# Attention and ternary FFN kernel: the product with v split in two pieces in steps without other matmul blocks

## The reference

```
q, k, v = x Wq' + bq, x Wk' + bk, x Wv' + bv      16 heads of 16
q, k    = rope(q) / 4, rope(k)
a       = softmax(q k') v                          per head, over 1024 keys
x       = layernorm(x + a Wo' + bo)
x       = layernorm(x + relu(x Q(W1)' + b1) Q(W2)' + b2)
```

## Time and profile before

| | us |
|---|---|
| runs: median (lowest to highest) | 3323.97 (3323.8 to 3325.73) |
| profiled execution: span from first to last instruction | 3316.4 |
| profiled execution: time around the span | not given by the page; the median of the runs is 7.5 above the span |
| PE busy | 3242.7 |
| DVE busy | 2990.2 |
| ACT busy | 2530.5 |
| POOL busy | 2147.2 |

### The profile page before, as it was taken

One profiled execution on the slowest core, in us unless ns is written; L12 is line 12 of the kernel. 1 busy time (PEld: TensorE's weight loads), 2 busy tenths in 40 slices (PEclk: granted clock), 3 DMA queues, 4 the chain that ended last, 5 costly groups with the idle time before them and its releaser, 6 DMA issues. The chain is left out here.

```text
span 3316.4 us, 81549 instructions
## 1 busy us (share of the span) xinstructions
PE 3242.7 (98%) x30726; PEld 1773.5 (53%) x30726; DVE 2990.2 (90%) x5721; ACT 2530.5 (76%) x4971; POOL 2147.2 (65%) x2440
## 2 busy tenths in 40 slices
PE   7989999999999999999999999999999999999997
PEld 4434555555555555555555555555555555544445
DVE  7888999999999999999999999999999999999965
ACT  3777777777777777777777777777777777777773
POOL 2575766766766766766766766766766776754435
PEclk7999999999999999999999999999999999999989
DMA  8444454454355345355355345345345345344211
GB/s 220 100 96 103 96 116 103 96 116 107 93 115 109 91 115 111 89 115 111 94 114 118 88 109 118 92 105 119 94 106 116 96 104 116 98 95 80 55 38 57
DMA packets 312553, 341.20 MB, mean 103 GB/s; under 512 B 77280, under 2 KB 260448, under 8 KB 312160
## 3 DMA queue, kind: packets, MB, share of 16 engines
q1 hardware_dynamic: 311584, 335.20, 44.2%
q10 hardware_dynamic: 576, 0.79, 0.2%
HBM read 195.37 MB, written 140.51 MB: 101 GB/s over the span
## 5 line engine op out<-in xcount | busy, mean ns | idle before, releaser
L1071 DVE TENSOR_REDUCE mxp<-ms 128x1 f32<-128x512 f32 x4064 | 2614.6, 681 | 245.5 <-PE ms L749 200.7
L897 ACT ACTIVATE prob<-sc 128x512 f32<-128x512 f32 x4096 | 2225.1, 597 | 655.4 <-PE sc L760 629.6
L760 PE MATMUL sc<-qa,ka 50*128 50x512 f32 x4096 | 1545.2, 444 | 27.5 <-ACT prob L897 27.1
L749 PE MATMUL ms<-ka,qa 48*128 48x512 f32 x4064 | 1536.7, 446 | 2.9 <-DVE mxp L1289 2.2
L760 PEld LDWEIGHTS sc<-qa,ka 50*128 50x128 f32 x4096 | 684.5, 185 | 1115.8 <-ACT prob L897 962.6
L777 PE MATMUL ob<-prob,v_sb 128*17 128x512 f32 x8192 | 1081.9, 600 | 2.4 <-ACT at_st L904 2.3
L749 PEld LDWEIGHTS ms<-ka,qa 48*128 48x128 f32 x4064 | 679.4, 185 | 10.4 <-DVE mxp L1071 4.5
L1402 POOL TENSOR_TENSOR ve<-mv,eps_sb 128x2 f32<-128x2 f32 x119 | 23.2, 195 | 493.1 <-DVE mv L1098 493.1
L1423 POOL TENSOR_TENSOR hid_r<-hid,hid_r 128x512 fp32r<-128x512 f32 x240 | 308.6, 1286 | 19.2
L777 PEld LDWEIGHTS ob<-prob,v_sb 128*17 128x17 f32 x8192 | 136.0, 95 | 258.4 <-issue 258.1
L597 PEld LDWEIGHTS job<-h_t,w_sb 64*128 64x128 f32 x3840 | 261.3, 186 | 23.4
(11 more groups left out here) (157 smaller groups left out, 2833.6 us busy)
## 6 DMA issues: line engine op xcount, KB each, us to landing
qk_parts<-parts SPq DMA_DIRECT2D x122, 512.0 KB, 4.2
ka<-qk_parts SPq DMA_DIRECT2D x378, 128.0 KB, 4.6
qa<-qk_parts SPq DMA_DIRECT2D x378, 128.0 KB, 7.4
attention<-at_st SPq DMA_DIRECT2D x128, 256.0 KB, 3.3
v_ones<-v_st SPq DMA_DIRECT2D x64, 272.0 KB, 2.4
v_sb<-v_ones SPq DMA_DIRECT2D x64, 272.0 KB, 8.5
xn<-x SPq DMA_DIRECT2D x64, 256.0 KB, 4.8
ao<-attention SPq DMA_DIRECT2D x128, 128.0 KB
```

Of the source, the lines that this page charges most:

```text
L749: nc.tensor.matmul(ms[upto(b, g, NS1, at) % MS_BANKS][:, :], operand(qa, b, g, j, ROWS)[:, qt * P:(qt + 1) * P], operand(ka, b, g, j, ROWS ...
L760: nc.tensor.matmul(sc[upto(b, g, HG * STEPS, n) % SC_BANKS][:, :], operand(ka, b, g, j, ROWS + MROWS)[:, tt * P:(tt + 1) * P], operand(qa, ...
L897: nc.scalar.activation(prob[st_ % 2][:, j, :], sc[upto(b, g, HG * STEPS, n) % SC_BANKS][:, :], ACT.Exp).then_inc(s["exp_done"], 1)
L1071: nc.vector.reduce_max(mxp[(b * G + g) % 2][:, kh, j * TT + qt:j * TT + qt + 1], ms[upto(b, g, NS1, at) % MS_BANKS][:, :], AX.X).then_inc( ...
```

## The change

In steps that have no job, W is made in two pieces of 256 queries each, the first behind S1 and the second behind S3. In steps with a job the order stays S0 S1 job S2 S3 W. Each piece has the four heads' matmuls with half the columns and loads the same v tile again. The `start` flag of an accumulation is set on the first piece alone, `stop` on the second; `pv_done` is told by the second piece. The waits at the head of `weigh` stand ahead of each piece.

```diff
-            def weigh(b, g, st_):
+            def weigh(b, g, st_, begin=0, end=NQ):
...
                 for j in range(HG):
-                    last = nc.tensor.matmul(ob[32 * j:32 * j + VW, :], v_sb[g % 2][:, tt, j, :], prob[st_ % 2][:, j, :],
-                                            start=(tt == 0), stop=(tt == TT - 1))
-                last.then_inc(s["pv_done"], 1)
-
-            def weigh_before(b, g, st_, first):
+                    last = nc.tensor.matmul(ob[32 * j:32 * j + VW, begin:end], v_sb[g % 2][:, tt, j, :], prob[st_ % 2][:, j, begin:end],
+                                            start=(tt == 0 and begin == 0), stop=(tt == TT - 1 and end == NQ))
+                if end == NQ:
+                    last.then_inc(s["pv_done"], 1)
+
+            def weigh_before(b, g, st_, first, begin, end):
 
                 if st_ > 0:
-                    weigh(b, g, st_ - 1)
+                    weigh(b, g, st_ - 1, begin, end)
                 elif not (first and g == 0):
-                    weigh(b + (g - 1) // G, (g - 1) % G, STEPS - 1)
+                    weigh(b + (g - 1) // G, (g - 1) % G, STEPS - 1, begin, end)
...
-                            if j == (3 if jobs else 1):
-                                weigh_before(b, g, st_, first)
+                            if jobs and j == 3:
+                                weigh_before(b, g, st_, first, 0, NQ)
+                            elif not jobs and j % 2 == 1:
+                                weigh_before(b, g, st_, first, j // 2 * (NQ // 2), (j // 2 + 1) * (NQ // 2))
```

## The result

| | before | after |
|---|---|---|
| median, us (lowest to highest) | 3324.85 (3323.8 to 3327.86), 4 runs | 3301.19 (3298.73 to 3303.37), 4 runs |
| profiled execution, us | not given | 3303.37 |
| its span, us | 3316.4 | 3301.6 |

The ratio is 0.9934, with a 95% interval of 0.9922 to 0.9947: faster by 0.7%.

The account below looks back on a forecast made before the run. PE and ACT take turns, neither full, with the whole product on their ring in 58 jobless steps. Gains of 8.0 (batch 0), 8.0 (five late groups) and 1.5 (last group) make 17.5 us: 3324.0 to 3306.5, range 3300 to 3316.

Parts of the forecast that it names:

- rival (c): Steps 5 to 8 of (15,3): denser steps may keep the clock up, time 3300.5 us; chance 0.08.
- Ring and price of a piece: PE-ACT cycle in jobless steps: 3.08 us falls to 2.65 a step, as a half piece costs 0.55 against 0.98 whole.
- Rival (b): Jobless steps: a piece costs 0.65 us, second piece adds 0.10 per step, time 3311; chance 0.21 together with rival (a).
- rival (d): Jobless steps: halving saves nothing, a piece takes 0.98 us, steps 0.2 longer, time 3335.5; chance 0.04.
- Rival (e): Jobless steps: an unseen wait keeps the score chain from being let go earlier, time 3321 to 3326 us; chance 0.07.
- the fixed part: Each piece of the product: 0.12 us that does not go with the clock, beside 0.43 for a half piece's columns.
- Batch 0 up to the gate: Jobless runs from (0,0) step 6 through (0,2) step 1: 3.7 us gained.
- The gate: Start of (0,3): POOL and the maxima's DMA cap the gain at 0 to 1 us, 0.4 taken; then 0.7 for steps 0-1.
- The five late groups: Groups (14,2) to (15,2): 1.6 us gained each, 8.0 in all, transposition in step 6 gated by POOL's norm.
- rival (a): Other engines take more: late groups 0.65 us each, batch 0 DMA waits give nothing, time 3312; chance 0.21 with rival (b).
- (15,3): Last group: 1.3 us from three steps before the clock halves, 0.2 from the cold steps, 1.5 in all.
- the 7.5 us around the span: Outside the profiled span: the runs' median lies 7.5 us above the span of 3316.4, kept unchanged in the forecast.

Follow-up runs that it names:

- first experiment: Kernel after, with both half pieces of the product placed behind the second score matmul: 3322.86 us, ratio 1.0006.
- early maxima: Kernel after, with POOL's splitting of the maxima for (0,3) put ahead of the last ternary piece in (0,2): 3302.48 us, ratio 0.9946.
- both halves early: Kernel after, both pairs of (0,3) maxima split ahead of the last ternary piece, on SP moved ahead of its ternary-weights wait: 3299.03 us, ratio 0.9928.
- uneven pieces: Kernel after, with the first piece of the product 320 queries and the second 192: 3303.12 us, ratio 0.9946.
- the control: Kernel before, with the moves of the maxima on POOL and SP at both places and no split of the product: 3323.09 us, ratio 0.9999.
- the small piece: Fastest kernel made, plus 64 queries of the product between third and fourth scores in steps 2 to 5 with a job: 3307.28 us, ratio 0.9961.

## Why the prediction was right, and where its terms were off

The direction, the mechanism and the range of 3300 to 3316 held. The narrower range of the forecast alone, 3302 to 3311, did not: the median of 3301.2 lies 0.8 below it, and nearer to the 3300.5 of rival (c) than to the forecast of 3306.5. The forecast lay 5.3 us above the median: the time around the span was taken 5.7 too long. Inside the steps wrong terms cancel.

- **Ring and price of a piece.** Forecast 2.65 a step and 0.55 a piece; measured 2.66 and 0.56. Rival (b), a piece at 0.65, falls, and so does rival (d), slower: a piece is far below the 0.88 from which PE's own sum decides. Rival (e) falls with the seven rows of the new step. But the fixed part was read wrongly: it belongs to the change from a product to a score and not to a piece (first experiment; the pieces of 320, 64 and 448 queries fit it too, at 0.66, 0.24 and 0.88 until the next score), and it came out right because in this order each piece is followed by a score. The ring I drew was one of two. With equal halves they are of equal length, so that the sum was right and the picture was half of it; the cut at 320 showed that.
- **How many steps.** 58, as counted.
- **Batch 0 up to the gate.** Forecast 3.7. Measured 4.24 at step 2 of (0,2), of which 0.86 arose before the first touched step: 3.4.
- **The gate.** Forecast: the gain at S0 of (0,3) is capped, 0.4. Measured 4.63 - 4.24 = 0.4. That POOL and the DMA of the maxima set it was right: with the maxima early the gain there is 7.25. What failed is the next term, 0.7 for steps 0 and 1 of (0,3) and no loss behind them. The steps ahead of the gate had gained 2.8 more by step 15, nearly all of it turned into PE standing still for 2.67 us, and behind that the clock fell. Steps 0 to 2 lost 2.45, where the same steps without the fall gained 0.82 (early maxima): the stretch cost 3.3. I had weighed a clock that might stay up, never one that might fall in a new wait. The experiment with both halves early gives the price of gate and clock together: 6 us.
- **(0,3), steps 8 to 15.** Forecast 3.2, measured 3.1.
- **The five late groups.** Forecast 1.6 each, measured 1.7 (14.47 - 5.93 = 8.54 for five). Steps 2 to 6 of the first group gave 1.33, steps 7 and 8 0.35. The transposition was gated by the norm as forecast, and by no more than forecast, so that this part of rival (a) falls. Its other part, gates of batch 0 that give nothing, came true there and cost more than (a) said.
- **(15,3).** Forecast 1.5, measured 3.8. I kept the length of the stretch at half clock; it was 10.2 us and not 17.1. Rival (c), a clock that stays up there, had 0.08. Put side by side, the traces (all but the one with the split in every step) say that this was too little: in steps 5 to 8 of (15,3) the five without the pieces at two places (two of the kernel before, both pieces behind S1, whole behind S3, the control) were all at half clock, for 17.1, 10.2, 10.2, 13.7 and 13.7 us; of the six with them, two were, for 10.2, and four not at all. Where it stayed up, the gain in (15,3) is 7.7 to 7.8 (uneven pieces, early maxima at one place and at both, the small piece) and not 3.8. So (c) comes about in a part of the executions. No run was made for this, and eleven traces are few; the one with the split in every step had the clock up there as well.
- **The sum of the steps.** Forecast 17.5. Measured 4.4 (batch 0) + 0.7 (a drift over the untouched batches, not explained) + 8.5 + 3.8 = 17.4. That it agrees is luck: -3.6 in batch 0, +2.3 in (15,3), +0.5 and +0.7.
- **Around the steps.** The span fell by 14.8 only: up to the first touched step it lost a net 1.0, and behind the last score 1.5; neither place has a changed instruction. Then the 7.5 us around the span: **this is the step that failed by size.** The profiled execution after took 3303.37 with a span of 3301.6, 1.8 around it, and every other execution whose span is on record shows 1.7 to 1.9. So the profiled execution before took about 3318.2 and was a fast one of its kernel; its span of 3316.4 and the 3324.0 are not of one execution. The repeated trace, 4.5 longer in span, shows one place where time goes: 3.85 behind the last score. By its own time the forecast is 3318.2 - 17.5 = 3300.7, against 3303.4 for the profiled execution after.

The gain by the run times is larger than by the steps. The two medians are 23.7 us apart, and the interval of the ratio says 18 to 26. The medians of the kernel before in the other comparisons are 3321.2, 3324.1 and 3320.1, 19 to 23 us above the 3301.2. The steps of the two traces account for 17.4 of it. Part of the difference is the clock, which each execution's mean shows: 47 executions of the kernel before, between 3315 and 3330 us, have it on record, and at 0.988, 0.989 and 0.990 they took 3323.6, 3321.3 and 3318.7 on average; the four of the kernel after took 3303.4, 3301.9 and, twice at 0.990, 3299.6 on average. At equal clock that is a gain of 19 to 20 us. What of the last 2 or 3 us is left beside the steps stays open.

## What to carry to other kernels

Where two engines take turns over two banks, draw every ring through both banks before placing a piece of work, and cut the piece so that the rings come out equal; a piece put where it looks free can lie on the other ring, as it did in the steps with a job. Ask of every shortened stretch what gate stands at its end: a wait of a few microseconds on a transfer costs itself and then the clock behind it, and the cure (here, issuing the maxima ahead of one piece of unrelated work) is worth nothing before the change and 6 us of steps after, of which the run times, at 2 us between the medians with intervals that overlap, can't yet show as much. Take a baseline from the execution whose trace is read, not from the median of others.

## What the runs showed of the hardware

- **Where the clock falls differs from run to run.** TensorE's granted clock was at half in the prologue for 44.4 or 47.8 us. Beyond that, place and length differ between traces of one and the same kernel: in (0,3) none and 3.4 us before, in (15,3) 17.1 and 10.2, behind it one stretch of 3.4 and three of 3.4 to 6.8. A stretch of 10.2 cost 3.3 us in (0,3), beside the same steps at full clock; in (15,3) having one or none made 4.0. The 12 us between runs of one kernel go with it: of the 47 executions of the kernel before, the 14 below 3320 us had a mean granted clock of 0.989 to 0.991, the 11 above 3325 one of 0.986 to 0.988. A mean lower by 0.001 is 6.6 us more at half clock, and such runs took 2.5 us longer (a fitted line, so an estimate; 2.4 to 2.6 in each of the three comparisons), 0.4 us for each microsecond at half.
- **A wait ahead of the fall.** Behind both waits of 2.6 to 2.7 us on the maxima the clock fell, and so it did behind the same wait with uneven pieces (2.56 us, then 13.7 at half). With the maxima early at both places it stayed up there. The Trainium skill (TensorE: Matmul & The Clock Gate, HAM oscillation) tells of waits on transfers, of some 3 to 5 us, that put the clock down; these rows agree, with shorter waits. But the fall at 231.6 in the repeated trace of the kernel before, and those in (15,3) with PE busy before them, came without such a wait. The one at 231.6, and two more in step 1 of (0,2) (177.4 with both pieces behind S1, 175.6 with uneven pieces), came within 2.3 us of the 1.1 us wait for the copies of `ob`; other traces have that wait and no fall. No run here shows why.
- **Eight more matmuls in four column strips cost next to nothing.** Up to the next score, sixteen of 256 columns took 0.99 and eight of 512 took 0.98. What costs is the change to the next score, 0.13 by the estimate above.
